# Causal self-attention of width 8: the next unit's first scores ahead of the shift, and masked exponentials cleared by VectorE in place of mask matmuls

## The reference

```python
def _L1_xattn_ref(x, cross_input, Wk, bk, Wq, bq, Wv, bv, ...):
    q = _heads(x @ Wq + bq)            # B, 16 heads, 256, 8
    k = _heads(x @ Wk + bk)
    v = _heads(x @ Wv + bv)
    att = jnp.einsum('bhqd,bhkd->bhqk', q, k) * scale
    causal = jnp.tril(jnp.ones((T, T), bool))
    att = jnp.where(causal[None, None], att, -jnp.inf)
    y = jnp.einsum('bhqk,bhkd->bhqd', jax.nn.softmax(att, axis=-1), v)
    ...                                # cross-attention with cross_input, added to y
    return y @ Wp + bp
```

## Time and profile before

| | us |
|---|---|
| median of 3 runs | 2622.39 (2617.27 to 2626.8) |
| profiled execution: its time | 2621.8 |
| profiled execution: its span | 2619.7 |
| PE busy in the span | 2204.5 (84%) |
| VectorE busy | 1823.9 (70%) |
| ScalarE busy | 1339.4 (51%) |
| GpSimd busy | 1244.3 (47%) |
| first and last shift of the changed phase start at | 416.3 and 739.5 |

### The profile page before, as it was taken

One profiled execution on the slowest core, in us unless ns is written; L12 is line 12 of the kernel. 1 busy time (PEld: TensorE's weight loads), 2 busy tenths in 40 slices (PEclk: granted clock), 3 DMA queues, 4 the chain that ended last, 5 costly groups with the idle time before them and its releaser, 6 DMA issues. The chain is left out here.

```text
span 2619.7 us, 68614 instructions
## 1 busy us (share of the span) xinstructions
PE 2204.5 (84%) x22578; PEld 1684.8 (64%) x22578; DVE 1823.9 (70%) x5026; ACT 1339.4 (51%) x2821; POOL 1244.3 (47%) x1952
## 2 busy tenths in 40 slices
PE   5859987999978678599999977899677999997845
PEld 3648984666656567477777755666554888885623
DVE  6975545666669745488888857677684666666977
ACT  3435552333334446355555545444544888883456
POOL 4446526555434465477777644333351434333333
PEclk9969998999989779799999989899876999998978
DMA  8022210000000223100000000000000121110000
GB/s 309 2 112 79 72 46 26 14 13 12 8 2 0 89 79 88 54 13 11 10 9 10 5 20 9 2 0 1 1 17 23 57 65 57 65 49 14 1 9 25
DMA packets 81633, 96.69 MB, mean 37 GB/s; under 512 B 16560, under 2 KB 60729, under 8 KB 79353
## 3 DMA queue, kind: packets, MB, share of 16 engines
q1 hardware_dynamic: 73216, 77.12, 9.1%
q0 software_dynamic: 8192, 16.79, 2.2%
HBM read 56.51 MB, written 37.36 MB: 36 GB/s over the span
## 5 line engine op out<-in xcount | busy, mean ns | idle before, releaser
L1931 DVE TENSOR_TENSOR l2f_experts_h_lo<-l2f_experts_h,l2f_experts_h_hi 128x512 fp32r<-128x512 f32 x256 | 186.7, 751 | 130.3 <-ACT l2f_experts_h_hi L1857 126.4
L991 POOL TENSOR_TENSOR a_pm<-a_pt,tri_post 128x256 f32<-128x256 f32 x256 | 179.1, 727 | 94.4 <-ACT a_pt L647 94.3
L785 DVE TENSOR_REDUCE l1s_negm<-l1s_s 128x3 bf16<-128x384 f32 x256 | 131.3, 557 | 108.2 <-PE l1s_s L476 108.1
L1872 ACT ACTIVATE l2f_experts_h<-l2f_experts_f,ahead 128x512 f32<-128x512 f32 x256 | 174.7, 687 | 51.3 <-DVE l2f_experts_h_lo L1931 45.9
L1969 POOL TENSOR_TENSOR l2f_acc<-l2f_experts_tmp,l2f_acc 128x512 f32<-128x512 f32 x64 | 82.8, 1294 | 228.3 <-DVE l2f_experts_tmp L1901 228.3
L785 DVE TENSOR_REDUCE a_negm<-a_s 128x2 bf16<-128x512 f32 x256 | 164.6, 685 | 32.7 <-PE a_s L476 32.1
L647 ACT ACTIVATE l1s_pt<-l1s_st 128x768 f32<-128x768 f32 x128 | 96.9, 811 | 158.5 <-PE l1s_st L511 158.5
L1857 ACT ACTIVATE l2f_experts_h_hi<-l2f_experts_h 128x512 fp32r<-128x512 f32 x256 | 154.2, 631 | 0.0
L647 ACT ACTIVATE a_pt<-a_st 128x1024 f32<-128x1024 f32 x128 | 126.5, 1066 | 2.8 <-PE a_st L511 2.8
L663 ACT ACTIVATE a_q_hi<-a_pa 128x256 fp32r<-128x256 f32 x64 | 24.6, 384 | 189.8 <-PE a_pa L442 189.8
L1792 PE MATMUL l2f_experts_f<-l2f_x_hi,l2f_experts_w_hi 128*128 128x512 f32 x256 | 100.7, 393 | 6.4 <-POOL l2f_experts_w_lo L1959 6.4
(11 more groups left out here) (549 smaller groups left out, 7056.7 us busy)
## 6 DMA issues: line engine op xcount, KB each, us to landing
expert_rows<-zeros SPq DMA_DIRECT2D x16, 1056.0 KB, 16.9
l2f_experts_wrow<-weights_by_expert SPq DMA_DIRECT2D x64, 256.0 KB, 3.1
l0f_w<-in_l0f_w SPq DMA_DIRECT2D x8, 640.0 KB
l0f_x_in_sb<-expert_rows SPq DMA_DIRECT2D x72, 64.0 KB
expert_rows<-l0f_y SPq DMA_DIRECT2D x72, 64.0 KB, 1.6
l1f_x_in_sb<-expert_rows SPq DMA_DIRECT2D x72, 64.0 KB
expert_rows<-l1f_y SPq DMA_DIRECT2D x72, 64.0 KB
ahead<-in_l2f_w SPq DMA_DIRECT2D x6, 512.0 KB, 4.7
```

Of the source, the lines that this page charges most:

```text
L785: dve.tensor_reduce(dst, src, AX.X, ALU.max, negate=True).then_inc(max_done, 1)
L991: last = pool.tensor_tensor(pm[:, par, heads_, kt, :], pt[:, par, heads_, kt * (T + P):kt * (T + P) + P], K["tri_post"][:].unsqueeze(1).br ...
L1872: act.activation(h[:, j], psum_f[j][:], ACT.Gelu, bias=col(e, j)).then_inc(h_ready, 1)
L1931: dve.tensor_tensor(h_lo[:, pos % 2, j], h[:, j], h_hi[:, pos % 2, j].bitcast(F32), ALU.subtract)\
```

## The change

The mask tile `mask_k` is gone, and with it the four mask matmuls a unit on the transposed scores. A tile `tri_upto` (128x128 fp32, one on and above the diagonal of key by query, zero below) takes its place in the set-up. After ScalarE has taken the exponentials of the diagonal blocks unmasked, VectorE clears what should be masked: `clear_later`, two operations a unit over the four heads' blocks, each `min(p, 3e38) * tri_upto`. The minimum turns an infinity into a finite number before it is multiplied by zero. `values` now waits for the clears of its unit. And in PE's stream the next unit's first mask and `scores(nn, half 0)` stand ahead of `shift(n)`, no longer behind it.

```diff
-            for name in ("mask_q", "mask_k"):
-                last = dve.memset(K[name][:], 0.0)
+            dve.memset(K["mask_q"][:], 0.0)
+            dve.memset(K["tri_upto"][:], 1.0)
...
-            select(K["mask_k"][:], ALU.is_ge, -1e30, 0, -1, [[-P, TT], [1, T]])
+            select(K["tri_upto"][:], ALU.is_ge, 0.0, 0, -1, [[1, P]])
...
             def shift(n, pos):
                 if before:
-                    for i in range(4):
-                        pe.matmul(psum_st[:, i, :].rearrange("p (j k) -> p j k", j=2)[:, :, 0:P], K["ident_bf"][:],
-                                  K["mask_k"][:, 0:1, 0:P].broadcast_to([P, 2, P]), start=False, stop=False,
-                                  skip_group_check=True)
                     pe.wait_ge(max_joined, n + 1)
...
                 if pm is not None:
                     pe.wait_ge(pm_ready, 2 * n + 2)
+                elif before:
+                    pe.wait_ge(pm_ready, n + 1)
...
+                if before and inside(nn):
+                    score_mask(nn, 0)
+                    scores(nn, bn, un, posn, 0)
                 if inside(n):
                     shift(n, pos)
                 if U == 1 and turn_now:
                     turn(b2, b2)
-                if inside(nn):
-                    if before:
-                        score_mask(nn, 0)
+                if inside(nn) and not before:
                     scores(nn, bn, un, posn, 0)
...
+            def clear_later(n, pos):
+
+                dve.wait_ge(exp_done, 2 * n + 2)
+                for col in (0, T):
+                    p = pt[:, pos % 2, :, col:col + P]
+                    last = dve.scalar_tensor_tensor(out=p, in0=p, scalar=3e38,
+                                                    in1=K["tri_upto"][:].unsqueeze(1).broadcast_to([P, 4, P]),
+                                                    op0=ALU.min, op1=ALU.mult)
+                last.then_inc(pm_ready, 1)
...
                     maxima(nn, posn, 3)
                     if before:
                         join_maxima(nn, posn)
+                if before and inside(n):
+                    clear_later(n, pos)
                 if paired and U == 1 and inside(n1):
```

More of the change, by code:

```diff
@@ L262, in constants @@
         "turn_p": sb("turn_p", [P, 1]), "step_e": sb("step_e", [P, NCH, NE]),
-        "mask_q": sb("mask_q", [P, TT, T], BF16), "mask_k": sb("mask_k", [P, TT, T], BF16),
+        "mask_q": sb("mask_q", [P, TT, T], BF16), "tri_upto": sb("tri_upto", [P, P]),
         "half": sb("half", [P, 8]), "own_slot": sb("own_slot", [P, 4]),
```

## The result

The changed kernel takes 2667.3 us (median of 4 runs, 2658.0 to 2671.2), the kernel before 2621.7 on the same chip (4 runs, 2617.3 to 2626.8). The ratio is 1.0173 [1.0147, 1.0200]: slower by 45.6 us. The profiled execution took 2671.2, its span 2669.2. The direction was forecast, and 55 us; the parts of that sum came out otherwise. `E` and the intervals 0 to 3 are those of the prediction.

The account below looks back on a forecast made before the run. The prediction saw PE and VectorE handing work back and forth in self-attention as the bound. It added 38 us for the units, 16 for contention and 1 at the end: 2622 + 55 = 2677 us, range 2634 to 2706.

Parts of the forecast that it names:

- `E` and the intervals 0 to 3: E ends a unit's second reduction pair; intervals run E to E, four a sequence: forecast 5.65, 5.27, 5.92, 6.3 us.
- The four units, sum 23.1, 38 us: Self-attention's four-unit sequence takes 23.1 us, 2.36 more than now; times 16 sequences, 38 us.
- The mask matmuls at nothing: Removing PE's four mask matmuls a unit, 38 us busy, saves nothing on the path: they run before the join ends.
- The moved scores would save 5.0 a sequence alone: Next unit's scores ahead of PE's shift: plain unit 3.86 instead of 4.83, four units 15.8, 5.0 us less a sequence.
- the first rival: Clears fit VectorE's idle gaps, only its work binds: 19.2 us a sequence, 1.6 less, total 2596; chance 0.09.
- the floor of 3.86: Plain unit with moved scores alone: the next reduction pair begins 0.90 after E, not 1.87, giving 3.86 us.
- Contention, 16 us: VectorE clears stretched beside GpSimd gathers (0.43) and key products (0.29): 1.2 us a sequence, 13 sequences, 16 us.
- the rival of whole-instruction blocking: Clears in units 3, 0, 1 wait for full gathers or products, key products for clears: 80 us, total 2702; chance 0.15.
- The clock, unpriced, left in the upper tail: PE's new gaps of 1 to 2 us might bring its granted clock below 1.00; no size or chance given.
- the 38 us by which PE's busy time was to fall: Expected sign in the self-attention stage: PE's busy time down by some 38 us.
- The hidden sequence change: Rival: V and keys arrive as early as before, VectorE alone binds, 21.2 us a sequence, total 2629; chance 0.14.
- Clears in the gaps: Clears fit VectorE's 115 us of idle time in the stage: 19.2 us a sequence, total 2596; chance 0.09.

Follow-up runs that it names:

- the kernel with gaps filled: Changed kernel plus twenty matmuls into an unused score-bank strip between mask and scores, in units opening with idle PE: 2627.7 us against the changed kernel's 2647.1; 1.0108 of before.
- the order alone: Kernel before with only the next unit's first mask and scores moved ahead of the shift, mask matmuls kept, no clears: 2638.0 us against 2595.2, ratio 1.0156.

## Why the prediction was right

Right in direction, in the time (2677 for 2667), and in where it goes: the queue of VectorE in plain units, PE's order and the late key product at the change of sequence. That the time came so near is luck in part: two terms were too large by 10 and 13 to 16 us, and a term that was left out, the clock, made up for most of it.

- **The four units, sum 23.1, 38 us.** Without the clock they add up to 22.33 on average in the kernel with gaps filled, 1.77 more than before's 20.56: 28 us, and the filling is in it. Interval 1 was forecast 5.27 and is 4.90, interval 2 5.92 and 5.48: VectorE sets them as said, but a clear alone is 0.685 and not 0.75, a pair 1.29 and not 1.40, and the operations behind it overlap (567.63 begins before the pair at 566.42 has ended, and the reductions at 568.26 before the transposition has). Interval 3 was forecast 6.3 and is 6.51, since scores start at E + 2.18 and not 2.0. Interval 0 was forecast 5.65 and is 5.56. V's layout at E + 5.19 was forecast at 5.2; the key product ends 1.55 after the new E (584.77), forecast 1.9.
- **The mask matmuls at nothing.** Right in the changed kernel's plain units, where VectorE binds. Where PE binds they count: the order alone has 7.20 in interval 3, with the masks gone it is 6.51.
- **The moved scores would save 5.0 a sequence alone.** Wrong: they save 0.14 in a plain unit and lose at the change of sequence, 32 us in all at full clock. The term wasn't in the sum, for VectorE set the units there, but the break-even of the first rival hung on it. The step that failed counted only what the first reductions wait for; the second pair waits for PE's whole load, 3.66, which no order shortens. With one clear and no masks a plain unit is 4.30, so the floor of 3.86 wasn't near even there.
- **Contention, 16 us.** The rows have it in length: a pair of 2.56 and one of 1.29, and a mean of 814 against a median of 685, some 16 us busy over 122 clears. But the term charged 0.43 for a gather, read from the 0.78 in the earlier trace rows, and a gather did nothing to the clears (0.68 to 0.74 beside one). That operation also ran 0.10 into a key product, and one before the stage, wholly beside a gather (395.92), took 0.35; what made the 0.78 stays open. The key products it is that held clears up. On the time it comes to less than 3 us: in intervals 3 and 0 another wait ends last. A single clear was thus held for as long as two products, as the rival of whole-instruction blocking has it, but that rival's key products did not move: the product at 584.15 starts as the gather ends and takes 0.62.
- **The clock, unpriced, left in the upper tail.** 18 us or a little more, shown by filling the gaps. By luck it took the place of the contention term in the sum: 28 + 18 = 46, and the stage grew by 45.0 and 46.3 in the two executions profiled. At full clock the sum of 55 would have met some 30. It also hid the 38 us by which PE's busy time was to fall: it fell by 4.
- **The hidden sequence change** (0.14) falls with V's layout at E + 5.19 and the gather behind it; without a gather, in the last two sequences, it was hidden.
- **Clears in the gaps** fall with a sequence of 22.33 at full clock against its 19.2.

## What to carry over

Before crediting an instruction moved forward, add up all that its engine must write between the same two handovers: an order changes which wait is last, not that sum. Price a collision by the wait that ends last in its interval, not by the stretched instruction. And when a change takes matmuls away or puts a wait at the head of PE's queue, look at the granted clock of the new gaps: here matmuls that compute nothing won back 18 of 46 us. The change itself still loses some 30 without the lower clock.

## What the hardware showed unexpectedly

PE's granted clock fell amid a stage in which PE was 79% busy (296 of 373), after gaps of 1.2 to 1.6 us; a single gap doesn't settle it: behind the idle 1.59 at 578.85 the shift still took 0.84, behind the 1.17 at 584.83 it took 1.46. Which sequences it hits varies between executions, and the sum hardly did in the two that were profiled: the stage was 45.0 and 46.3 us longer.

A three-operand VectorE operation of 512 columns with both inputs in SBUF took 685 ns in the median, about the 693 of the two-operand one. Beside a gather it took 0.68 to 0.74, beside two key products up to 1.95; two writes of 175 columns a head in the same place took 1.38, as they did elsewhere (609.10). The Trainium skill (SBUF — State Buffer, Who interferes with whom) has a two-input VectorE operation and a GpSimd operation that reads SBUF exclude each other. The clears agree with it where they met key products, which read the keys from SBUF; the writes, which have no SBUF input, were not held up.
